# A six-layer transformer kernel: the three up-projections of the feed-forward part trade the PSUM banks they write

## What is computed

```python
def ffn_layer(x, g, bln, W1, b1, W2, b2):
    mu = x.mean(-1, keepdims=True)
    var = ((x - mu) ** 2).mean(-1, keepdims=True)
    xn = (x - mu) / jnp.sqrt(var + 1e-05) * g + bln
    hg = xn @ W1 + b1
    a, gate = jnp.split(hg, 2, -1)
    return a * jax.nn.gelu(gate, approximate=False) @ W2 + b2
for i in range(DEPTH):
    x = attn_layer(shift_tokens(x), Wqkv[i], q_scale[i], k_scale[i], Wo[i]) + x
    x = ffn_layer(shift_tokens(x), ln_g[i], ln_b[i], W1[i], b1[i], W2[i], b2[i]) + x
```

## Time and profile before

| | |
|---|---|
| median of 3 runs | 1886.04 us (1882.17 to 1889.05) |
| the profiled execution's own time | 1887.05 us |
| its span | 1885.2 us |
| granted TensorE clock, mean | 0.964 of 2.4 GHz |
| busy share of the span | PE 89%, PEld 63%, DVE 84%, ACT 65%, POOL 79% |

### The profile page before, as it was taken

The page is one execution under the profiler, slowest core; times in us unless marked ns, Lnnn a source line. Parts: engine busy times, 40 slices in busy tenths (PEclk is TensorE's granted clock), DMA queues, the critical chain, the costliest instruction groups (busy, mean ns, idle before and its releaser), DMA issues. The chain is left out here.

```text
span 1885.2 us, 76475 instructions
## 1 busy us (share of the span) xinstructions
PE 1674.5 (89%) x30960; PEld 1193.9 (63%) x30960; DVE 1578.2 (84%) x2345; ACT 1221.7 (65%) x2072; POOL 1483.0 (79%) x819
## 2 busy tenths in 40 slices
PE   3946878899999999999999999999999999999974
PEld 2523556666766676667667666676676766776663
DVE  5787767789889898898998888989989889898854
ACT  3334556567677776777777767777767677776753
POOL 1638767778888888888888888888888888888841
PEclk8878989999999999999999999999999999999997
DMA  3001131122223222323221332222242223222210
GB/s 133 1 1 45 49 99 48 47 67 60 63 74 104 58 56 64 78 69 89 64 67 45 87 102 67 67 53 70 67 111 57 54 67 78 66 58 65 67 47 23
DMA packets 80698, 121.88 MB, mean 65 GB/s; under 512 B 16776, under 2 KB 29574, under 8 KB 79750
## 3 DMA queue, kind: packets, MB, share of 16 engines
q1 hardware_dynamic: 80646, 121.14, 24.4%
HBM read 19.36 MB, written 1.05 MB: 11 GB/s over the span
## 5 line engine op out<-in xcount | busy, mean ns | idle before, releaser
L729 PE MATMUL r<-wqkv,xs 128*128 (+1 forms) x1152 | 561.2, 618 | 13.0 <-DVE rot_sin L1246 3.7
L1433 POOL TENSOR_TENSOR rot<-rot,root 128x1024 f32<-128x1024 f32 x192 | 377.9, 1988 | 120.6 <-DVE root L1284 120.6
L1405 POOL TENSOR_TENSOR rot<-rot,rot_sin 128x1024 f32<-128x1024 f32 x192 | 451.8, 2365 | 1.2 <-DVE rot_sin L1246 1.2
L729 PEld LDWEIGHTS r<-wqkv,xs 128*128 128x128 f32 x1152 | 210.5, 196 | 213.0 <-issue 197.6
L1079 ACT ACTIVATE squares<-r 128x512 f32<-128x512 f32 x384 | 217.6, 598 | 83.9 <-PE r L729 82.8
L1235 DVE TENSOR_TENSOR rot<-r,table 128x1024 f32<-128x1024 f32 x192 | 232.7, 1212 | 23.0 <-PE r L734 10.2
L1418 POOL TENSOR_TENSOR squares<-squares 128x512 f32<-128x512 f32 x192 | 244.8, 1275 | 9.0 <-ACT squares L1079 8.8
L1449 POOL TENSOR_TENSOR probs<-probs,rinv 128x1024 f32<-128x1024 f32 x96 | 182.8, 1905 | 81.0 <-DVE rinv L1306 81.0
L1246 DVE TENSOR_TENSOR rot_sin<-r,table 128x512 f32<-128x512 f32 x384 | 242.6, 672 | 0.0
L734 PE MATMUL r<-square,rot 128*128 128x128 f32 x1536 | 208.1, 279 | 19.5 <-POOL rot L1433 14.0
L734 PEld LDWEIGHTS r<-square,rot 128*128 128x128 f32 x1536 | 169.5, 141 | 83.8 <-issue 29.9
(11 more groups left out here) (125 smaller groups left out, 2688.5 us busy)
## 6 DMA issues: line engine op xcount, KB each, us to landing
vwin<-vtok SPq DMA_DIRECT2D x576, 128.0 KB, 2.3
vwin<-vtok SPq DMA_DIRECT2D x384, 64.0 KB, 2.0
wqkv<-in_wqkv SPq DMA_DIRECT2D x6, 1536.0 KB, 8.3
wo<-in_wo SPq DMA_DIRECT2D x6, 512.0 KB, 4.9
w<-in_w SPq DMA_DIRECT2D x6, 341.0 KB, 3.0
x<-in_x SPq DMA_DIRECT2D x4, 256.0 KB, 3.7
rope<-in_rope SPq DMA_DIRECT2D x1, 1024.0 KB
out_x<-y SPq DMA_DIRECT2D x4, 256.0 KB, 2.3
```

The source lines that it names most:

```text
L729: pe.matmul(dst[:, c * 512:(c + 1) * 512], xs1[:, u, :], w.rearrange("p a n -> p (a n)"), start=True, stop=True).then_inc(S[done], 1)
L1405: pool.tensor_tensor(r, r, rot_sin[:, k, :, :, :].rearrange("p h a d -> p h (a d)"), ALU.add)\
L1433: pool.tensor_tensor(r, r, bcast(root[:, at:at + HEADS], 2, DH), ALU.mult)\
```

## The change

Up-projections 0, 1 and 2 write pm_norm, pm_out, pm_norm before, and pm_out, pm_norm, pm_out now; the Gelus and gates read them there. The waits that protect the banks follow. With all pairs running:

| work of TensorE | waited for | waits for |
|---|---|---|
| up-projection 0 | second residual of pair m-5 (`x_ready`) | squaring of pair m-3 (`xc_squared`) |
| up-projection 1 | squaring of pair m-3 | second residual of pair m-5 |
| up-projection 2 | first gate of pair m-4 | the same |
| output projection | second gate of pair m-4 | third gate of pair m-4 |
| spread of the roots | third gate of pair m-4 | second gate of pair m-4 |

The diff's core (TensorE's step, then a line each of ScalarE's and VectorE's; branches that run only near the two ends are left out):

```diff
                 if runs(m - 4):
-                    if runs(m - 5):
-                        pe.wait_ge(S["x_ready"], PPL + m - 4)
...
+                    if runs(m - 3):
+                        pe.wait_ge(S["xc_squared"], m - 2)
...
-                    ff_up(m - 4, 0, pm_norm)
+                    ff_up(m - 4, 0, pm_out)
...
                 if runs(m - 4):
-                    if runs(m - 3):
-                        pe.wait_ge(S["xc_squared"], m - 2)
...
+                    if runs(m - 5):
+                        pe.wait_ge(S["x_ready"], PPL + m - 4)
...
-                    ff_up(m - 4, 1, pm_out)
+                    ff_up(m - 4, 1, pm_norm)
...
                     pe.wait_ge(S["gated"], 3 * (m - 4) + 1)
-                    ff_up(m - 4, 2, pm_norm)
+                    ff_up(m - 4, 2, pm_out)
...
                 if runs(m - 2):
                     if runs(m - 4):
-                        pe.wait_ge(S["gated"], 3 * (m - 4) + 2)
+                        pe.wait_ge(S["gated"], 3 * (m - 4) + 3)
...
                     out_project(m - 2)
...
                 if runs(m - 3):
                     if runs(m - 4):
-                        pe.wait_ge(S["gated"], 3 * (m - 4) + 3)
-                    elif runs(m - 4):
-                        pe.wait_ge(S["gated"], 3 * (m - 4) + 1)
+                        pe.wait_ge(S["gated"], 3 * (m - 4) + 2)
...
                     spread_rstd(m - 3)
...
-                    ff_gelu(m - 4, 0, pm_norm)
+                    ff_gelu(m - 4, 0, pm_out)
...
-                    ff_gate(m - 4, 0, pm_norm)
+                    ff_gate(m - 4, 0, pm_out)
```

More of the change, by code:

```diff
@@ L869, in step @@
                 if runs(m - 4):
-                    if runs(m - 5):
-                        pe.wait_ge(S["x_ready"], PPL + m - 4)
+                    if runs(m - 3):
+                        pe.wait_ge(S["xc_squared"], m - 2)
                     elif runs(m - 3):
-                        pe.wait_ge(S["refined"], ROOT_OPS * (m - 1) + 2)
-                    else:
-                        pe.wait_ge(S["hatted"], m - 3)
-                    ff_up(m - 4, 0, pm_norm)
+                        pe.wait_ge(S["residual1"], m - 2)
+                    elif runs(m - 5):
+                        pe.wait_ge(S["gated"], 3 * (m - 5) + 3)
+                    elif runs(m - 5):
+                        pe.wait_ge(S["gated"], 3 * (m - 5) + 1)
+                    else:
+                        pe.wait_ge(S["xc_squared"], m - 3)
+                    ff_up(m - 4, 0, pm_out)
                 if runs(m - 1):
@@ L910, in step @@
                 if runs(m - 4):
-                    if runs(m - 3):
-                        pe.wait_ge(S["xc_squared"], m - 2)
+                    if runs(m - 5):
+                        pe.wait_ge(S["x_ready"], PPL + m - 4)
                     elif runs(m - 3):
-                        pe.wait_ge(S["residual1"], m - 2)
-                    elif runs(m - 5):
-                        pe.wait_ge(S["gated"], 3 * (m - 5) + 2)
-                    else:
-                        pe.wait_ge(S["xc_squared"], m - 3)
-                    ff_up(m - 4, 1, pm_out)
+                        pe.wait_ge(S["refined"], ROOT_OPS * (m - 1) + 2)
+                    else:
+                        pe.wait_ge(S["hatted"], m - 3)
+                    ff_up(m - 4, 1, pm_norm)
                 if runs(m - 1):
@@ L971, in step @@
                     if runs(m - 4):
-                        pe.wait_ge(S["gated"], 3 * (m - 4) + 2)
+                        pe.wait_ge(S["gated"], 3 * (m - 4) + 3)
+                    elif runs(m - 4):
+                        pe.wait_ge(S["gated"], 3 * (m - 4) + 1)
                     elif runs(m - 3):
@@ L1026, in step @@
                     elif runs(m - 5):
-                        pe.wait_ge(S["gated"], 3 * (m - 5) + 3)
-                    elif runs(m - 5):
-                        pe.wait_ge(S["gated"], 3 * (m - 5) + 1)
+                        pe.wait_ge(S["gated"], 3 * (m - 5) + 2)
                     elif runs(m - 6):
@@ L1187, in step @@
                 if runs(m - 4):
-                    ff_gelu(m - 4, 1, pm_out)
-                    ff_gelu(m - 4, 2, pm_norm)
+                    ff_gelu(m - 4, 1, pm_norm)
+                    ff_gelu(m - 4, 2, pm_out)
                 if runs(m - 2):
@@ L1354, in step @@
                 if runs(m - 4):
-                    ff_gate(m - 4, 1, pm_out)
+                    ff_gate(m - 4, 1, pm_norm)
                 if runs(m - 1):
@@ L1360, in step @@
                 if runs(m - 4):
-                    ff_gate(m - 4, 2, pm_norm)
+                    ff_gate(m - 4, 2, pm_out)
                 if runs(m):
```

## The result

The changed kernel takes 1944.74 us (median of 4 runs, 1943.57 to 1950.57), the kernel before 1887.55 in the 4 runs beside it. The ratio is 1.031, with a 95% interval of 1.0274 to 1.0346: slower, by 57 us, as forecast (1944.3).

A forecast was written before the change was run, and what follows sets the result against it. A loop from first residual through roots, query transpose and output projection was taken to set 41 equal steps of 34.12 us. 57.0 + 1.3 = +58.3 us on 1887.05 gives 1945.4, against the median 1944.3 us; range 1924 to 1962.

The forecast's parts named there:

- The removed wait is worth 0: First up-projection starts 1.25 us earlier, but the query's transpose still waits for GpSimd: 0, within 0.1 us a step.
- A: Rival, not slower: the query's transpose moves up by as much as 1.25 us a step; about 1880 to 1886; chance 0.02.
- The output projection: 1.00 + 0.29 + 0.10 = 1.39 us a step: Output projection waits for the third gate: gate's lateness, hand-over and slower start from an empty engine; 57.0 us in 41 steps.
- B: Rival, less slower: unseen slack in the loop, say VectorE's residual to roots, swallows half; +30, 1916 us; chance 0.05.
- The clock: TensorE's clock in the 41 steps: stays at 1.00 despite a second gap; the sum has nothing for it.
- C: Rival, slower still: TensorE's clock falls at each output projection, 1.66 us more a step, 68 us: 2012; chance 0.06.
- The ends, +1.3 us: Outside the equal steps: steps 4 to 6 0, step 48 +3.3, steps 50 and 51 -2.0; between -2 and +5.

The follow-up runs named there:

- e1: The kernel before with one count changed, so the output projection waits for the third gate, banks as they were: 1947.84 us, ratio 1.0318.
- e5: The kernel before (old banks and waits) with VectorE's third gate moved up right behind the second: 1888.83 us, ratio 1.0.
- e2: The changed kernel with VectorE's third gate moved up right behind the second: 1883.36 us, ratio 0.9974 to the kernel before.
- e4: The changed kernel with VectorE's third gate one place later, behind the sum of squares of the keys: 1962.65 us, ratio 1.0409 to the kernel before.
- e6: e2 with VectorE's row sums and reciprocal of the second block placed before the first residual: 1867.24 us, ratio 0.9902 to the kernel before.
- e8: The changed kernel with only the row sums of the second block placed before the first residual: 1893.91 us, ratio 1.0059 to the kernel before.
- e7: The kernel before with only the row sums of the second block placed before the first residual: 1875.35 us, ratio 0.9956.
- e11: e6 with ScalarE's second-key squares ahead of staging the residual and VectorE's second-query sum of squares behind the first residual: 1824.31 us.
- e12: e11 with the banks and waits of the kernel before: 1826.08 us, ratio 0.9665 to the kernel before.

## Why the prediction was right

**The removed wait is worth 0.** Right for the 41 steps, and shown twice where the wait really holds the up-projection back, for 1.25 us a step: e1 against the change, and e5 against e2. The time from the roots' end to the turned query is 2.04 us in the kernel before and 2.03 in the change; the 0.1 us that was allowed on either side was not needed. A (the removed wait pays back the new one) is out. TensorE's wait for GpSimd's product rose by 63.8 us and not by some 50: it is 1.40 us a step, since the up-projection ahead of it is over sooner and lasts 1.03 us in place of 1.13. That the wait is worth exactly nothing rests on two sizes that tie here: wait and up-projection together end where GpSimd's product does. With a shorter product it would be worth something, which no run tried.

**The output projection: 1.00 + 0.29 + 0.10 = 1.39 us a step.** Measured 1.37 (35.52 - 34.14): the gate's end to the start is 0.28 where 0.29 was taken, and the projection takes 3.72 in place of 3.62. 41 steps took 56.3 us more, 57.0 were forecast. B (slack in the loop) is out for this change, since e4's further delay came through in full; but e6 to e8 show that the stretch behind the residual has branches, and a change there would have met them. The prediction also put the adds ahead of the roots in this stretch without saying why; the last section has what ties them.

**The clock.** 1.00 in the 41 steps. The Trainium skill's rule in "TensorE: Matmul & The Clock Gate", on a clock that swings when TensorE pauses between groups ("A second HAM failure mode: psum-queue depth-cycling"), did not come true with gaps of 1.1 and 1.4 us in a step, nor in e4 with 1.6 and 1.4; C is out.

**The ends, +1.3 us.** Three stretches make up the ends in the two profiled executions.

To the first residual of step 6 the change is 3.1 us shorter, where 0 was forecast. This is no effect of the edit: 3.9 us of it are there at the first residual of step 2 (222.4, not 226.3), and the banks and waits that differ are used from step 4 on. There the clock was down from 217.4 to 220.8 us in the trace of before and not in that of after. Over all kernels the first residual of step 6 lies between 373.6 and 390.5 us; those with row sums first are shorter from step 2 to step 6 (152.0 to 159.2 us, the others 160.2 to 167.0).

From the first residual of step 47 to that of step 48 the change takes 8.1 us more (42.55, not 34.41), where the forecast has 4.7, the later start of the projection. The third gate itself ended 3.2 us later behind the first of these residuals than in the trace of before: with the clock at 1.2 GHz from 1856.2 to 1863.0 us, which began while TensorE idled 3.21 us for GpSimd's product, the transposes at the head of the step took 1.94 us where such a group takes 1.09. And the clock was down again from 1873.2 to 1883.5, so the projection took 5.74 (5.28 in the earlier trace rows). The sum had no term for the clock there. All nine kernels with the new banks have the low clock at the head of step 48, and of the five with the old banks two (e1 and e7); no run tells whether the banks cause it.

From there to the end of the last computing instruction the change takes 4.8 us less (53.9, not 58.7), where the forecast has 3.4 less: 1.37 for the transposes that need not wait for GpSimd, and 2.0 for the freed up-projections. The latter was too small: e2 against e5 has 5.3 us less there, and e5 does not differ from e2 in the gate.

Together -3.1 + 56.3 + 8.1 - 4.8 = 56.5, which is what lies between the two profiled executions. That the forecast hit to 0.4 us is luck: these terms happen to cancel, and the four runs lie 7 us apart for the change and 10 for the kernel before. The 1.37 us a step are not luck.

## What to carry to other kernels

A wait that is moved is to be judged by what comes next behind it in the queue: here 51 us of idle time vanished from one line and reappeared at the next, because GpSimd's product ended at the same moment as the delayed up-projection. Draw the loop that closes a step before pricing a wait, and look for the releaser's place in its own queue: moving one half-microsecond instruction of VectorE into idle time undid the 57 us that the new bank assignment cost. And when the loop is shortened in one place, look for the branch beside it; the row sums alone gave 0.28 us a step, with the branch repaired 1.40.

## What the runs showed of the hardware that was not expected

VectorE's operation L1274, which makes the first guess of the roots, takes 2.21 us on 128x67 elements in the steps and 0.20 in step 48. The trace of after has it beside GpSimd's adds:

```profile
959.67 4.68 POOL L1405 TENSOR_TENSOR rot<-rot,rot_sin 128x1024 f32<-128x1024 f32 x2
...
962.20 2.21 DVE L1274 TENSOR_SCALAR root<-minus_half 128x67 int32<-128x67 int32 x1
```

It ends at 964.41, 0.06 us after the adds (964.35), and 0.05 to 0.06 after them in every one of the 41 steps of all kernels but e11 and e12; in these two it starts behind them and takes 0.20, and L1261, which now falls into the second add, takes 2.1 us and ends 0.05 after it. The Trainium skill, in "SBUF — State Buffer", section "Who interferes with whom", says that VectorE and GpSimd share a pair of ports, and that where both need it, as a tensor_scalar of VectorE can, the one that issues first holds it for its whole instruction while the other stands still. The traces agree, and by that reading GpSimd's adds are a link of the loop here, though VectorE waits for no semaphore of theirs. A busy VectorE was in part a waiting one. What the step would gain if these operations did not fall beside the adds was not tried. An estimate from these rows is 2.21 - 0.20 = 2.0 us for L1274, and the bound is GpSimd's idle time of 2.50 us before the product.

A second point: the delay from the third gate's end to the output projection was 0.28 us in each of the 41 steps of the change, of e1, e4 and e8. The first up-projection, whose released wait is also the first of three, had 0.29 in the earlier trace rows. So in this loop the hand-over could be taken from another place of the same shape.
